# Forward transform along w on eight array tiles instead of four, with the image order of half the stored spectrum repaired by the loads

## What is computed

```python
h = layer_norm(x @ fc0_w + fc0_b, ln0_g, ln0_b)            # the stem, 32 channels
for i in range(4):                                          # the layers
    x_ft = jnp.fft.rfft2(h)                                 # only 12 + 12 rows and 12 columns are used
    out_ft[:, :, :M1, :M2] = einsum('bixy,ioxy->boxy', x_ft[:, :, :M1, :M2], w1)
    out_ft[:, :, -M1:, :M2] = einsum('bixy,ioxy->boxy', x_ft[:, :, -M1:, :M2], w2)
    h = irfft2(out_ft) + conv_1x1(h)
    h = layer_norm(h); if i < 3: h = gelu(h)
h = fc3(gelu(fc2(gelu(fc1(h)))))                            # the head
...
h = h + attention(layernorm(h)); h = h + experts(layernorm(h))
```

## Time and profile before

| | |
|---|---|
| time, median of 3 runs | 5650.85 us (5644.83 to 5652.54) |
| the profiled execution | 5642.42 us, its span 5640.7 us |
| granted PE clock, mean | 0.970 |
| PE busy | 5186.8 us, 92% of the span |
| DVE, ACT busy | 3918.7 us and 3869.3 us, 69% each |
| POOL busy | 638.0 us, 11% |
| DMA | 756.30 MB, mean 134 GB/s |

### The profile page before, as it was taken

How to read it: one execution, slowest core, us unless ns; L and a number is a source line. 1 busy time by engine, 2 the same in 40 slices (tenths; PEclk the granted TensorE clock), 3 DMA queues, 4 the chain that set the end, 5 groups by cost and what they waited for, 6 DMA issues and landing times.

```text
span 5640.7 us, 134571 instructions
## 1 busy us (share of the span) xinstructions
PE 5186.8 (92%) x43556; PEld 2937.8 (52%) x43556; DVE 3918.7 (69%) x7712; ACT 3869.3 (69%) x6261; POOL 638.0 (11%) x943
## 2 busy tenths in 40 slices
PE   5888899999999999999999999999999999868778
PEld 3444556666666666666666654433333333334443
DVE  5888888888888888888888865555545555455454
ACT  5888776888666888666888656677777777523333
POOL 0133100333000333000333000000000000000000
PEclk9999999999999999999999999999999999878888
DMA  1334467666677666777676752221111111000000
GB/s 68 126 137 150 147 197 229 213 225 223 211 234 223 217 220 226 218 228 230 213 230 215 230 156 65 75 57 53 52 51 47 51 53 53 13 4 4 7 7 4
DMA packets 397184, 756.30 MB, mean 134 GB/s; under 512 B 245041, under 2 KB 303410, under 8 KB 331322
## 3 DMA queue, kind: packets, MB, share of 16 engines
q1 hardware_dynamic: 377402, 704.04, 39.2%
q0 software_dynamic: 19456, 48.01, 3.7%
HBM read 397.49 MB, written 354.42 MB: 133 GB/s over the span
## 4 chain that ended last, share of the span: by engine, by line
PE 76%; ACT 7%; DVE 7%; issue 6%; SPq 1%; DMA 1%; ACTq 1%; DVEq 0%
PE ps_y L920 11%; PE ps_t L932 9%; PE ps_t L1026 8%; PE ps_t L941 7%; PE ps_f L920 7%; PE ps_y L912 5%; PE ps_f L1011 4%; PE ps_s L897 3%; PE ps_s L970 3%; PE ps_s L957 3%; PE ps_t L1035 2%; PE ps_y L996 2%; PE ps_t L349 2%; PE ps_y L886 2%; ACT wslot L1205 2%
## 5 line engine op out<-in xcount | busy, mean ns | idle before, releaser
L1332 DVE TENSOR_REDUCE big<-big 128x16 f32<-128x512 f32 x1280 | 853.6, 674 | 683.1 <-ACT big L1170 678.5
L1325 DVE TENSOR_TENSOR big<-big 128x512 f32<-128x512 f32 x1280 | 939.0, 764 | 30.2 <-DVE big L1354 18.8
L1170 ACT ACTIVATE big<-ps_y 128x512 f32<-128x512 f32 x892 | 546.3, 612 | 465.6 <-PE ps_y L920 418.4
L932 PE MATMUL ps_t<-ident,big 128*128 128x128 f32 x5120 | 798.4, 279 | 54.4 <-DVE big L1325 25.2
L1186 ACT ACTIVATE big<-ps_t,g_now 128x512 f32<-128x512 f32 x1024 | 821.9, 803 | 4.3 <-PE ps_t L932 3.1
L920 PEld LDWEIGHTS ps_y<-conv_now,big 128*128 128x128 f32 x5088 | 617.2, 191 | 362.8 <-issue 362.8
L1179 ACT ACTIVATE big<-ps_t 128x512 f32<-128x512 f32 x1024 | 634.5, 620 | 213.6 <-PE ps_s L957 145.9
L932 PEld LDWEIGHTS ps_t<-ident,big 128*128 128x128 f32 x5120 | 568.6, 141 | 345.2 <-issue 303.6
L941 PE MATMUL ps_t<-ident,big 128*128 128x128 f32 x4096 | 647.4, 281 | 90.8 <-ACT big L1179 88.6
L920 PE MATMUL ps_y<-conv_now,big 128*128 128x128 f32 x5088 | 717.9, 284 | 0.0
L941 PEld LDWEIGHTS ps_t<-ident,big 128*128 128x128 f32 x4096 | 454.8, 142 | 280.6 <-issue 154.8
(11 more groups left out here) (197 smaller groups left out, 7326.3 us busy)
## 6 DMA issues: line engine op xcount, KB each, us to landing
hstore<-big SPq DMA_DIRECT2D x256, 1024.0 KB, 4.1
big<-hstore SPq DMA_DIRECT2D x256, 1024.0 KB, 5.3
xmodes<-x_out SPq DMA_DIRECT2D x128, 312.0 KB, 4.4
y_kt<-ymodes SPq DMA_DIRECT2D x512, 78.0 KB
ymodes<-y_st SPq DMA_DIRECT2D x192, 144.0 KB, 2.5
mix_room<-xmodes SPq DMA_DIRECT2D x48, 336.0 KB, 6.8
mix_room<-xmodes SPq DMA_DIRECT2D x48, 288.0 KB, 5.9
ymodes<-y_st SPq DMA_DIRECT2D x64, 192.0 KB, 3.3
```

The costliest lines, as they stand in the source:

```text
L932: last = nc.tensor.transpose(ps_t1[:, 128 * b:128 * b + 128], y_sb[2 * k + wh][:, 128 * b:128 * b + 128], ident[:, :])
L1170: af(y_sq[wh], of[:, wh, :], ACT.Square).then_inc(s["sq_done"], 1)
L1325: v_.tensor_tensor(groups(y_sb[2 * k + wh]), groups(y_sb[2 * k + wh]), rstd[:, k // 2, at:at + 16].unsqueeze(2).to_broadcast([128, 16, 32] ...
L1332: v_.tensor_reduce(ss[:, k // 2, at:at + 16], groups(y_sq[wh]), AX.X, ALU.add).then_inc(s["ss_done"], 1)
```

## The change

In `fwd_w` the output rows of the second spectrum half are exchanged between the two images of a pair: `32 * (image ^ sx)` in place of `32 * image`. The eight matmuls then use eight different tiles (row half, column quarter) of the array, where before the four tiles of `sx` = 0 were used again by `sx` = 1. What lies in `xmodes` for c = 2 and 3 has the images of each pair swapped. The loads of `mix_room` put them right: for these c one DMA becomes two, one for each image of the pair, each with half of the runs. The semaphore counts go from 64 to 96, since a chunk half is now six DMAs.

```diff
-            return xm[half][32 * c:32 * c + 32, :, :], src[c][:, :, m0:m1]
+            dst = xm[half][32 * c:32 * c + 32, :, :]
+            if c < 2:
+                return [(dst, src[c][:, :, m0:m1])]
+            return [(dst.rearrange("p (s i) m -> p i s m", i=2)[:, image],
+                     src[c].rearrange("p (s i) m -> p i s m", i=2)[:, 1 - image, :, m0:m1]) for image in range(2)]
...
                 for c in range(COMP):
-                    sp.dma_start(*modes_part(half, chunk, c)).then_inc(x_half[half], 16)
+                    for dst, src in modes_part(half, chunk, c):
+                        sp.dma_start(dst, src).then_inc(x_half[half], 16)
...
-                pool.dma_start(*modes_part(half, 0, c)).then_inc(x_first[half], 16)
+                for dst, src in modes_part(half, 0, c):
+                    pool.dma_start(dst, src).then_inc(x_first[half], 16)
...
-                            r, at = slice(64 * image, 64 * image + 64), 64 * j + 32 * image
+                            r, at = slice(64 * image, 64 * image + 64), 64 * j + 32 * (image ^ sx)
...
-                        pe.wait_ge(x_first[part // 2], 64 * (ph + 1))
+                        pe.wait_ge(x_first[part // 2], 96 * (ph + 1))
                     else:
-                        pe.wait_ge(x_half[part // 2], 64 * (3 * (ph if chunk == 1 else ph - 1) + chunk))
+                        pe.wait_ge(x_half[part // 2], 96 * (3 * (ph if chunk == 1 else ph - 1) + chunk))
```

## The result

The changed kernel takes 5610.65 us (median of 4 runs, 5597.16 to 5614.13), the kernel before, measured beside it, 5651.69 us (4 runs, 5644.83 to 5653.74). The ratio is 0.9925, 95% interval 0.9907 to 0.9942: about 41 us less (by the interval 33 to 53), where 59 were forecast.

What follows compares the result with a forecast made beforehand. PE was taken to bound the layers, ACT and DVE the stem. Layer quads save 67.9 us, less 8.5 us of waits for loads: 59.4 us off the median 5650.85 gives 5591 us, range 5574 to 5614.

Steps and rivals of the forecast that it cites:

- the forecast itself: Whole kernel: a gain of 45 to 75 us, given a chance of 0.74.
- the signs that were named for being wrong: Load groups visibly over 4.1 to 4.7 us, landings beyond 10.3 us, clock falling in the stem, or `fwd_w` keeping four rounds.
- I take a saving of 0.70 us for one `fwd_w`: Each `fwd_w`: two rounds instead of four on eight tiles, 0.72 or 0.70 us saved by two estimates.
- Layer quads: 97 x 0.70: 97 `fwd_w` in layer-type quads each pass on the full saving, 67.9 us in all.
- 14 places ... 8.5 us: Layer-type quads: at 14 of 18 places PE arrives before `h_in` lands, turning 8.5 us of saving into waits.
- rival 1: Two extra DMAs add 0.7 us each at 21 load places: 14.5 us more lost, 5606 us; chance 0.09.
- I take 0 for the delay: Split mode loads on SP: the two extra DMAs do not push out the landing of the next load; 0 us.
- the bound of 0.7 us: Split mode loads: each extra DMA costs its shortest issue, 0.344 us; 0.7 us at 18 + 3 places, 14.5 us.
- Stem quads: nothing ... Both waits only grow: Stem: the shorter `fwd_w` saves nothing, only lengthening waits of DVE for ACT's queue and PE for ACT; bound 9.8 us gain.
- Rival 4: Part of the saving goes to another engine or the stem's lower clock, up to 27 us: 5618 us; chance 0.06.

Runs made afterwards that it cites:

- after_again: The changed kernel measured once more, with nothing altered: 5606.89 us, ratio 0.9918 to the kernel before.
- tiles_only: The kernel before with only the eight tiles in `fwd_w`, its four loads left, so half the spectrum mixes swapped images: 5614.7 us, ratio 0.9933.
- late_loads: The changed kernel with SP's groups of mode loads issued one body later, behind the load of `h_in`: 5599.59 us, ratio 0.9910 to the kernel before.
- split_only: The kernel before with only the loads split for c = 2 and 3, images in old order, four tiles: 5652.94 us, ratio 1.0000.
- stem_twice: The changed kernel with the eight `fwd_w` matmuls issued twice in the stem, same result: 5602.61 us, ratio 0.9916 to the kernel before.
- late_thrice: The changed kernel with mode loads behind the load of `h_in` and the stem's `fwd_w` matmuls issued three times: 5571.43 us, ratio 0.9863.
- late_twice_2: Second measurement of the changed kernel with mode loads behind the load of `h_in` and the stem's `fwd_w` matmuls issued twice: 5585.69 us, ratio 0.9881.
- before_late: The kernel before with only SP's groups of mode loads issued one body later, behind the load of `h_in`: 5637.89 us, ratio 0.9966.
- late_twice: The changed kernel with mode loads behind the load of `h_in` and the stem's `fwd_w` matmuls issued twice: 5580.34 us, ratio 0.9883.
- late_fill: The changed kernel with mode loads behind the load of `h_in` and the stem's `fwd_w` and `fwd_h` matmuls each issued twice: 5580.25 us, ratio 0.9870.

## Why the prediction was right or wrong

The time, 5610.65 us, lies in the range of 5574 to 5614, near its end. The gain of 41 us is under the 45 to 75 that were called the forecast itself, and one of the signs that were named for being wrong came true: the clock fell in the stem.

- **"I take a saving of 0.70 us for one `fwd_w`": right.** The slot fell from 1.56 to 0.88 us, 0.68. The distance of two `fwd_w` in the layers' quads with weights went from 25.26 to 24.58 us (medians). The strided operand costs 0.02 us at most beyond the 0.86 of `fwd_h`'s form.
- **"Layer quads: 97 x 0.70", less 8.5 for the landings: right.** From n = 32 to 128 lie 96 quads, 96 x 0.70 - 8.5 = 58.7; measured 55.8 (2498.8 to 2443.0), and 54.9 in `after_again`.
- **"14 places ... 8.5 us": right.** (The listed spare times give 1.4 us at the 14 places, so 8.4; and 8 of the 18 have no time to spare, not 14 as rival 1 says.) Waits for `hstore` went from 1.7 us at 2 places to 10.0 at 15. In `tiles_only`, with four loads, they are 11.3 us at 15 places, so it is PE's earlier arrival and not the split. Removing the 11.1 us of `after_again` gave the layers 5.6 us in `late_loads`, where 3.9 us of waits for `y_kt` were new.
- **"I take 0 for the delay": right for the landing, wrong in its reason for the issue.** The issue of a group did get longer, by 1.03 us, more than the bound of 0.7 us; but the landing, counted from the group's start, stayed at 13.7 us. `split_only` at 1.0000 settles that it costs nothing.
- **"Stem quads: nothing ... Both waits only grow": this step failed.** PE's waits there are not spare time that costs nothing: PE stood longer, its clock fell, the records behind the idle time took longer, and ACT, which bounds the stem, waited 11.4 us more for them. The cost of the stem was 17.2 us by the first profile and 8.4 by the second. `stem_four`, which leaves the stem on four tiles, gains 57 us: the rest of the sum holds without this term. Rival 4 named the mechanism, with up to 27 us if the clock's loss doubles and a chance of 0.06. The loss did double, from 0.07 to 0.14, but cost 12.2 us over the 16 quads, since the clock acts only where ACT waits for PE. The evidence was in the window that the prediction quoted, 0.93 in a quad where PE waits 1.25 us: a stage whose clock is already below full may answer to more idle time. It should have been a term of the sum. With 17 us the sum gives 42, where 41 were measured; with the 8 us of the second profile it gives 51. So the close match of the first is in part luck; a single profile does not fix the term better than that.
- The remaining 12.6 us between the profiled executions lie behind the layers, in attention and experts, where both kernels have the same code. They are one stretch of attention, between the same two instructions of ACT, which took 35.8 us in the kernel after and 23.1 before, at granted clocks of 0.57 and 1.00. `split_only`, which runs at the time of the kernel before, has a stretch of 35.2 us at 0.56, and so does `after_again`; `stem_twice`, on eight tiles, has none. So it does not come with the change. What decides whether an execution has one was not found. After, then before:

```profile
5065.50:5101.30 35.80, 33.34 (x98) 16.76 (x98) 12.43 (x29) 9.35 (x12) 0.00 (x0) 0.57 0.00 0
```

```profile
5104.60:5127.70 23.10, 20.19 (x98) 10.03 (x98) 11.83 (x28) 9.14 (x13) 0.00 (x0) 1.00 0.00 0
```

## What to carry to other kernels

Taking work from PE in a stage that PE does not bound can cost time: where a window shows a granted clock below full, look up how long the bounding engine waits for PE there, price the added idle time as slower PE work in those waits, and try the change with that stage left as it was. Where one stage gains and another loses, apply the edit by stage (`stem_four`), or fill PE's waits with repeated work that nobody waits for (`late_thrice`), and look at the clock of the window and not at the time alone. When a wait for one DMA is removed by a new order, look at once for the DMA that has become the last in the queue.

## What the runs showed of the hardware

- Sixteen records that used eight array tiles and two banks, both row halves writing each bank, took 0.88 us to the next matmul; on four tiles 1.56 us. The shared bank costs nothing that these rows show. The rule of the Trainium skill that the prediction weighed (TensorEngine Tiling (Array Packing), Restrictions and Gotchas, PSUM Pressure), read as holding for a whole bank, does not hold for them. But within one column quarter the two row halves write different banks here (`64 * j + 32 * (image ^ sx)` with bank `sx`), and so they do in `fwd_h`; whether they could share a bank in the same quarter no run shows.
- Two changes that both act on PE's idle time in the stem were worth more together than apart: 27 us against 4 and 7 by time, 21 against 5 and 1 in the stem of the profiles, with the clock over the last eight stem quads at 1.00 against 0.96 and 0.94.
- The same 4096 runs in six DMAs in place of four took SP 1.03 us more to issue, with the landing of the next load unchanged.
- PE stands still with no wait in the profile at the place where the layers' loop is entered again (and once more for 2.5 to 3.4 us where the layers end, in all kernels). There the timeline of the kernel before has

```profile
1679.17 0.65 PE L941 MATMUL ps_t<-ident,big 128*128 128x128 f32 x4 [2.00 <-issue]
```

and the changed kernel 2.02 us at its place, 1.76 when measured again. `late_twice_2` there has two such gaps, and the low clock behind the first:

```profile
1644.51 1.11 PE L947 MATMUL ps_t<-ident,big 128*128 128x128 f32 x4 [3.24 <-issue]
...
1648.53 0.48 PE L938 MATMUL ps_t<-ident,big 128*128 128x128 f32 x1 [2.26 <-issue]
```

The body between two `fwd_w` takes 34.7 us there against 28.9 before. The nine profiles of kernels in which PE's stem has its old number of matmuls have 1.8 to 2.7 us (2.26 in `late_loads` and 2.68 in `before_late`, so the order of the loads makes little of it). Those with more matmuls in the stem have 4.04 and 2.12 (`stem_twice`), 3.34 and 2.12 (`late_twice`), 4.97 (`late_fill`), but 1.52 in `late_thrice`. So it changes with the stem's code for PE, but not with its length in an even way; the cause stays open. The layers as a whole are at most 3.4 us longer for it.
